# A two-layer residual kernel: VectorE adds the bias of another sequence of each group, at another place in its order

## The chip, the cores and the metric

The kernel runs on one core of a Trainium2 chip. A core has TensorE (PE in the profile), which multiplies matrices into the PSUM banks; VectorE (DVE), ScalarE (ACT) and GpSimd (POOL), which work elementwise; and SyncE (SP), which here only issues DMAs. Each engine runs its own instructions in order, and they wait for one another through semaphores. The metric is device time in microseconds (us): the median over the runs of one kernel.

## The reference, cut to what matters

There are 64 sequences of 128 rows and 512 columns, in float32. Two layers follow each other, each with a residual:

```
attn   = tanh(x @ W1 + b1); scores = attn @ v
p      = softmax(scores under a prefix, postfix or cloze mask, chosen per sequence)
x      = x + (p @ x) / cnt                       # first layer
x      = x + (x @ W[cat] + b[cat])               # second layer, W and b chosen per sequence
```

## The kernel before, in words

**The products.** With M the 128x128 matrix I + p/cnt of a sequence, the output is M @ (x @ (W[cat] + I)) plus the bias row b[cat]. So each sequence k needs x @ (W + I), called `xw(k)`, and then M @ that, called `pz(k)`; both sum into the same PSUM bank `ps_y`, of which there are five. Every float32 operand is split into a rounded high part and the remainder (`_hi` and `_lo`, float32r), and three products of the parts stand for one: 12 matmuls for `xw`, 3 for `pz`.

**The groups.** The sequences come in 16 groups of four; b = k % 4 is the place in the group. W1, the scores, the softmax and the transposed M are computed once for a group (`hidden`, `scores_group`, `exp_group`, `scale_group`, `transpose_probs`, `split_mix`). The order of every engine is written out by hand: a prologue, and then a loop over k in which each step of an engine stands where the code puts it. TensorE's iteration k does `xw(k)`, `pz(k-2)`, and for b = 0 the transposes, for b = 1 `hidden(g+1)` and for b = 2 `scores_group(g+1)`.

**Who does what.** W comes in 1 MB loads into five `w_raw` buffers. The identity is added to it by VectorE (`add_identity`, L466), for b = 1 and 2 by GpSimd (L282). ScalarE rounds it (`split_w_hi`, L346), and VectorE takes the remainder (`split_w_lo`, L479). The same pair works on x for `hidden` (L336, L472), on the first product (`z_hi` L382, `z_lo` L507), on the attention vector (`av_hi` L354, `av_lo` L484) and on the mixing matrix (`mix_hi` L375, `mix_lo` L502). GpSimd's second identity of a group waits for `av_lo`, its first for a `w_lo`. Further links of the softmax are VectorE's masked maximum (L492), ScalarE's exponentials (L361), GpSimd's `row_div` (L324), VectorE's reciprocal `row_scale` (L498) and ScalarE's scaling (L368).

**The bias.** For three sequences of a group the bias is a fourth matmul of `pz` (L695), and ScalarE copies the bank to `out_sb` (`copy_out`, L388). For one of them, the one with b = `WIDE`, SP loads the bias row into `out_sb[WIDE]`, spread over 128 partitions (`load_wide`, L240), and VectorE's `add_wide` (L514) adds the bank to it; then `pz` has three matmuls and ScalarE copies nothing. `wait_out` sends whoever needs the result (the store of k on SP, L234, and `xw(k+5)` on TensorE, which reuses the bank) to the right semaphore.

**SP's queue.** At t it issues `store(t-3)`, for b = 3 `load_x(g+3)` (1 MB, L230), `load_wide(g)` at its place, and `load_w(t+7)` (L219), which waits until the `w_lo` that used that buffer is done.

Of the kernel before, what the change touches and what calls it, by code (L numbers as in the profile page):

```python
# [39 lines left out]
def program(nc, xg, ids, w1, w, bias, out):  # L40
    GROUPS, P, DC, GS = xg.shape
# [6 lines left out]
    assert A == P and w1.shape[1] == DC * A + 2 and D == DC * P and C == P // 2  # L48
    HALF = DC // 2
    NX, NT, NW, NH, NL, NZ, NO, NY = 3, 2, 5, 4, 3, 3, 4, 5  # L50
    WIDE = 1
    assert NO == G
    RAW = 6

# [1 line left out]
    with ctx:  # L56
# [120 lines left out]
        def w_count(k):  # L177

            return k - RAW + 1
# [5 lines left out]
        def by_pool(k):  # L185

            return k > 3 * G and k % G in (1, 2)
# [9 lines left out]
        def wide(k):  # L197
            return k % G == WIDE

        def wait_out(engine, k):  # L200

            if wide(k):
                engine.wait_ge(sum_ready, k // G + 1)
            else:
                engine.wait_ge(out_ready, k - (k + G - WIDE - 1) // G + 1)

        @block.sync
        def _(sp):
            def load_cat(k):
                return sp.value_load(ids_row[0:1, k:k + 1], min_val=0, max_val=C - 1)  # L210

            def load_w(k, cat=None):
                if cat is None:
                    cat = load_cat(k)
                if k - NW >= RAW:
                    sp.wait_ge(w_lo_ready, w_count(k - NW))
                elif k >= NW:
                    sp.wait_ge(xw_done, k - NW + 1)
                sp.dma_start(w_raw[k % NW][:], w[bass.ds(cat, 1)].rearrange("a p c h -> p (a c) h"))\  # L219
                    .then_inc(w_in[k % NW], 16)  # L220

            def load_x(g):
                if g == NX:
                    sp.wait_ge(xw_done, G)
                elif g > NX:
                    if g == NX + 1:
                        sp.wait_ge(xw_done, RAW)
                    sp.wait_ge(xT_lo_ready, g - NX)
                    sp.wait_ge(pre_done, g - NX + 1)
                sp.dma_start(x_raw[g % NX][:], xg[g]).then_inc(x_in[g % NX], 16)  # L230

            def store(k):
                wait_out(sp, k)
                sp.dma_start(out[k], out_sb[k % NO][:]).then_inc(out_stored[k % NO], 16)  # L234

            def load_wide(g):
                cat = load_cat(G * g + WIDE)
                if g >= 1:
                    sp.wait_ge(out_stored[WIDE], 16 * g)
                sp.dma_start(out_sb[WIDE][:], bias[bass.ds(cat, 1), :].to_broadcast([P, D])).then_inc(wide_in, 16)  # L240

            sp.dma_start(ids_row[:], ids.rearrange("(a n) -> a n", a=1)).then_inc(ids_in, 16)
            for h, c in enumerate(halves):
                sp.dma_start(x_raw[0][:, c, :], xg[0][:, c, :]).then_inc(x0_in[h], 16)
            sp.wait_ge(ids_in, 16)
            cat_2 = load_cat(2)
            sp.wait_ge(w_in[0], 16)
            load_w(2, cat_2)
            load_x(1)
            load_w(3)  # L250
            sp.dma_start(b_raw[0:C, :], bias).then_inc(b_low_in, 16)
            sp.dma_start(b_raw[C:P, :], bias).then_inc(b_high_in, 16)
            load_w(4)
            load_w(5)
            load_x(2)
            load_w(6)
            load_wide(0)

            for t in range(B + 3):
                g, b = t // G, t % G  # L260
                if t >= 3:
                    store(t - 3)
                if b == 3 and g + 3 < GROUPS:
                    load_x(g + 3)
                if b == 2 and 1 <= g < GROUPS:
                    load_wide(g)
                if t + 2 + NW < B:
                    load_w(t + 2 + NW)
            for slot in range(NO):
                sp.wait_ge(out_stored[slot], 16 * (B // NO + (1 if slot < B % NO else 0)))  # L270
# [59 lines left out]
        def _(act):  # L330
# [40 lines left out]
            def split_mix_hi(g):  # L371
                act.wait_ge(probsT_done, g + 1)
                if g >= 2:
                    act.wait_ge(pz_done, G * (g - 1))
                nc.scalar.activation(mix_hi[g % 2][:], ps_pT[:].rearrange("p (b j) -> p b j", b=G), ACT.Copy)\  # L375
                    .then_inc(mix_hi_ready, 1)

            def split_z_hi(k):
                act.wait_ge(xw_done, k + 1)
                if k >= NZ:  # L380
                    act.wait_ge(pz_done, k - NZ + 1)
                nc.scalar.activation(z_hi[k % NZ][:], ps_y[k % NY][:], ACT.Copy).then_inc(z_hi_ready, 1)  # L382

            def copy_out(k):
                act.wait_ge(pz_done, k + 1)
                if k >= NO:
                    act.wait_ge(out_stored[k % NO], 16 * (k // NO))
                nc.scalar.activation(out_sb[k % NO][:], ps_y[k % NY][:], ACT.Copy).then_inc(out_ready, 1)  # L388
# [27 lines left out]
            split_z_hi(4)  # L416
            split_w_hi(6)
            split_mix_hi(1)
            copy_out(2)
            split_z_hi(5)  # L420
            split_w_hi(7)
            copy_out(3)
# [8 lines left out]
            for k in range(2 * G, B + 3):  # L431
                g, b = k // G, k % G
# [20 lines left out]
        def _(dve):  # L453
            eye = ident[:].rearrange("p (a j) -> p a j", a=1)

            def diagonal(slot):
                return w_raw[slot][:].rearrange("p c (i j) -> p (c i) j", j=P)[:, ::DC + 1, :]
# [6 lines left out]
            def add_identity(k):  # L464
                dve.wait_ge(w_in[k % NW], 16 * (k // NW + 1))
                nc.vector.tensor_tensor(diagonal(k % NW), diagonal(k % NW), eye.to_broadcast([P, DC, P]), ALU.add)\  # L466
                    .then_inc(wi_ready, 1)

            def split_xT_lo(g):
                dve.wait_ge(xT_hi_ready, g)  # L470
                cols = split_columns(g)
                nc.vector.tensor_tensor(xT_lo[g % NT][:, :, cols], x_raw[g % NX][:, :, cols],  # L472
                                        xT_hi[g % NT][:, :, cols].bitcast(F32), ALU.subtract).then_inc(xT_lo_ready, 1)

            def split_w_lo(k):
                dve.wait_ge(w_hi_ready, w_count(k))
                if k - NL >= RAW:
                    dve.wait_ge(xw_done, k - NL + 1)
                nc.vector.tensor_tensor(w_lo[k % NL][:], w_raw[k % NW][:], w_hi[k % NH][:].bitcast(F32),  # L479
                                        ALU.subtract).then_inc(w_lo_ready, 1)  # L480
# [15 lines left out]
            def row_scale_group(g):  # L496
                dve.wait_ge(div_ready, g + 1)
                nc.vector.reciprocal(row_scale[:], row_div[:]).then_inc(scale_ready, 1)  # L498

            def split_mix_lo(g):  # L500
                dve.wait_ge(mix_hi_ready, g + 1)
                nc.vector.tensor_tensor(mix_lo[g % 2][:], ps_pT[:].rearrange("p (b j) -> p b j", b=G),  # L502
                                        mix_hi[g % 2][:].bitcast(F32), ALU.subtract).then_inc(mix_lo_ready, 1)
# [6 lines left out]
            def add_wide(g):  # L510
                k = G * g + WIDE
                dve.wait_ge(pz_done, k + 1)
                dve.wait_ge(wide_in, 16 * (g + 1))
                nc.vector.tensor_tensor(out_sb[WIDE][:], ps_y[k % NY][:], out_sb[WIDE][:], ALU.add)\  # L514
                    .then_inc(sum_ready, 1)
# [57 lines left out]
            add_identity(6)  # L573
            row_scale_group(1)
            split_xT_lo(2)
            add_wide(0)
            add_identity(7)
            split_z_lo(4)
            split_w_lo(6)
            split_mix_lo(1)  # L580
            add_identity(8)
            split_w_lo(7)
            split_z_lo(5)
# [10 lines left out]
            for k in range(2 * G, B + 1):  # L594
                g, b = k // G, k % G
                if b == 3 and g + 1 < GROUPS:
                    max_group(g + 1)
                if b == 1 and g + 1 < GROUPS:
                    split_xT_lo(g + 1)
                if k + 2 < B:  # L600
                    split_w_lo(k + 2)
                if b == 1 and g < GROUPS:
                    split_mix_lo(g)
                if b == 2 and g + 1 < GROUPS:
                    split_av_lo(g + 1)
                split_z_lo(k - 1)
                if b == 0:
                    add_wide(g - 1)
                if k + 4 < B and not by_pool(k + 4):
                    add_identity(k + 4)  # L610
                if b == 3 and g + 1 < GROUPS:
                    row_scale_group(g + 1)

        @block.tensor
        def _(pe):
# [151 lines left out]
```

## Time and profile before

| | |
|---|---|
| median of 3 runs | 310.32 us (310.23 to 310.41) |
| the profiled execution | 311.67 us, of which 309.9 us are the span of the trace |
| TensorE busy | 302.9 us, 98% |
| VectorE busy | 278.1 us, 90% |
| ScalarE busy | 262.3 us, 85% |
| GpSimd busy | 86.0 us, 28% |
| DMA | 105.69 MB, mean 341 GB/s |
| chain that ended last | TensorE 88%, "issue" 6% |

The span is the time from the first to the last record of the core. The busy share of TensorE counts matmuls whose records overlap, so that it says little on how closely they follow one another; the distance between two starts says that. From about 60 us on, until 285 us, every group repeats the one before it.

### The profile page before, as it was taken

The page shows a single profiled execution, that of the slowest core. Times are in us where ns is not written, and L with a number is a line of the kernel's source. Part 1 is how long each engine was busy: PE and PEld are TensorE (multiplying, and loading weights), DVE is VectorE, ACT ScalarE, POOL GpSimd, SP SyncE. Part 2 cuts the span into 40 slices and gives each one's busy share as a digit, 9 for nine tenths or more (in the row PEclk, how much of TensorE's full clock was granted, in tenths as well). Part 3 has the DMA queues.
Part 4 walks back from the last instruction along what each step waited for, and adds up shares of the span by engine and source line. Part 5 has one row for each costly group of instructions (what it writes and reads, how often), then busy time and mean ns, then how long its engine had stood idle before and what let it go on. Part 6 is the DMA issues. An engine that isn't in the chain of part 4 may idle for free.

```text
span 309.9 us, 4890 instructions
## 1 busy us (share of the span) xinstructions
PE 302.9 (98%) x1284; PEld 233.7 (75%) x1284; DVE 278.1 (90%) x385; ACT 262.3 (85%) x429; POOL 86.0 (28%) x119
## 2 busy tenths in 40 slices
PE   8999999899999999999999999999999999999995
PEld 4445478588787878878788887888878787887884
DVE  4247699999999999999999999999999999999961
ACT  2254978989999898999989899998999999899952
POOL 5020400334132243413234341323424133302100
PEclk9999999999999999999999999999999999999999
DMA  7999899999999999999999999999999999986133
GB/s 257 404 389 412 339 403 379 415 396 295 352 373 318 404 320 401 363 354 373 327 406 319 408 350 361 361 322 409 323 392 349 370 378 334 399 327 224 67 135 135
DMA packets 23516, 105.69 MB, mean 341 GB/s; under 512 B 2625, under 2 KB 2626, under 8 KB 13378
## 3 DMA queue, kind: packets, MB, share of 16 engines
q1 hardware_dynamic: 23058, 103.03, 89.3%
q10 hardware_dynamic: 432, 2.36, 1.9%
q8 instruction: 10, 0.16, 0.2%
q14 instruction: 16, 0.13, 0.1%
HBM read 88.61 MB, written 16.78 MB: 340 GB/s over the span
## 4 chain that ended last, share of the span: by engine, by line
PE 88%; issue 6%; ACT 2%; DMA 2%; POOLq 1%; DVE 0%; SPq 0%; POOL 0%; ACTq 0%
PE ps_y L677 17%; PE ps_y L679 17%; PE ps_y L678 17%; PE ps_pre L636 13%; PE ps_y L689 4%; PE ps_y L690 4%; PE ps_y L691 4%; PE ps_y L695 3%; PE ps_pT L653 2%; PE ps_y L665 2%; PE ps_pre L625 2%; DMA x_raw<-in_x 2%; PE ps_scores L646 1%; PE ps_scores L644 1%; ACT probs L361 1%
## 5 line engine op out<-in xcount | busy, mean ns | idle before, releaser
L479 DVE TENSOR_TENSOR w_lo<-w_raw,w_hi 128x2048 fp32r<-128x2048 f32 x58 | 135.1, 2330 | 0.9 <-ACT w_hi L346 0.9
L346 ACT ACTIVATE w_hi<-w_raw 128x2048 fp32r<-128x2048 f32 x58 | 111.6, 1926 | 7.5 <-POOL w_raw L282 7.5
L677 PE MATMUL ps_y<-w_hi,xT_hi 128*128 128x512 f32 x232 | 91.7, 395 | 0.0
L679 PE MATMUL ps_y<-w_hi,xT_lo 128*128 128x512 f32 x232 | 90.5, 390 | 0.0
L678 PE MATMUL ps_y<-w_lo,xT_hi 128*128 128x512 f32 x232 | 90.3, 389 | 0.0
L282 POOL TENSOR_TENSOR w_raw<-w_raw,ident 128x512 f32<-128x512 f32 x26 | 33.6, 1294 | 113.5 <-DVE w_lo L479 75.0
L679 PEld LDWEIGHTS ps_y<-w_hi,xT_lo 128*128 128x128 f32 x232 | 43.5, 188 | 9.4
L507 DVE TENSOR_TENSOR z_lo<-ps_y,z_hi 128x512 fp32r<-128x512 f32 x64 | 43.7, 684 | 7.7 <-ACT z_hi L382 7.7
L678 PEld LDWEIGHTS ps_y<-w_lo,xT_hi 128*128 128x128 f32 x232 | 43.6, 188 | 8.8
L382 ACT ACTIVATE z_hi<-ps_y 128x512 fp32r<-128x512 f32 x64 | 38.8, 607 | 13.3 <-PE ps_y L679 5.1
L677 PEld LDWEIGHTS ps_y<-w_hi,xT_hi 128*128 128x128 f32 x232 | 43.6, 188 | 8.6
L289 POOL COPY mask<-penalty 128x128 bf16 x64 | 43.9, 716 | 9.4 <-issue 9.3
L472 DVE TENSOR_TENSOR xT_lo<-x_raw,xT_hi 128x2048 fp32r<-128x2048 f32 (+1 forms) x15 | 33.2, 2214 | 0.3 <-ACT xT_hi L336 0.3
L388 ACT ACTIVATE out_sb<-ps_y 128x512 f32<-128x512 f32 x48 | 29.0, 605 | 2.0 <-PE ps_y L695 2.0
L324 POOL TENSOR_TENSOR row_div<-row_sum,seen 128x4 f32<-128x4 f32 x16 | 6.4, 398 | 81.3 <-ACT probs L361 81.3
L336 ACT ACTIVATE xT_hi<-x_raw 128x2048 fp32r<-128x2048 f32 (+1 forms) x15 | 28.1, 1870 | 0.0
L689 PE MATMUL ps_y<-z_hi,mix_hi 128*128 128x512 f32 x64 | 25.9, 405 | 0.1
L466 DVE TENSOR_TENSOR w_raw<-w_raw,ident 128x512 f32<-128x512 f32 x37 | 25.3, 684 | 0.0
L690 PE MATMUL ps_y<-z_hi,mix_lo 128*128 128x512 f32 x64 | 24.9, 389 | 0.0
L691 PE MATMUL ps_y<-z_lo,mix_hi 128*128 128x512 f32 x64 | 24.9, 389 | 0.0
L352 ACT ACTIVATE attn<-ps_pre,w_pack 128x512 f32<-128x512 f32 x16 | 11.0, 690 | 15.8 <-PE ps_pre L625 8.0
L361 ACT ACTIVATE probs<-ps_scores,neg_max 128x128 f32<-128x128 f32 x64 | 22.4, 362 | 2.2 <-DVE neg_max L492 2.2
(70 smaller groups left out, 378.3 us busy)
## 6 DMA issues: line engine op xcount, KB each, us to landing
w_raw<-in_L_cond_W SPq DMA_DIRECT2D x62, 1024.0 KB, 8.4
out<-out_sb SPq DMA_DIRECT2D x64, 256.0 KB, 6.2
x_raw<-in_x SPq DMA_DIRECT2D x15, 1024.0 KB, 7.3
out_sb<-in_L_cond_b SPq DMA_DIRECT2D x16, 256.0 KB, 5.6
w_raw<-in_L_cond_W ACTq DMA_DIRECT2D x2, 1024.0 KB, 7.5
x_raw<-in_x SPq DMA_DIRECT2D x2, 512.0 KB, 5.2
w_pack<-in_W_b_v ACTq DMA_DIRECT2D x1, 257.0 KB, 2.8
b_raw<-in_L_cond_b SPq DMA_DIRECT2D x2, 128.0 KB, 8.2
```

The source lines that it names most:

```text
L289: last = nc.gpsimd.tensor_copy(mask[g % 2][:, i:i + 1, :], penalty[:, bass.ds(kind, 1), :])
L346: nc.scalar.activation(w_hi[k % NH][:], w_raw[k % NW][:], ACT.Copy).then_inc(w_hi_ready, 1)
L382: nc.scalar.activation(z_hi[k % NZ][:], ps_y[k % NY][:], ACT.Copy).then_inc(z_hi_ready, 1)
L479: nc.vector.tensor_tensor(w_lo[k % NL][:], w_raw[k % NW][:], w_hi[k % NH][:].bitcast(F32), ALU.subtract).then_inc(w_lo_ready, 1)
L507: nc.vector.tensor_tensor(z_lo[k % NZ][:], ps_y[k % NY][:], z_hi[k % NZ][:].bitcast(F32), ALU.subtract).then_inc(z_lo_ready, 1)
L636: last = nc.tensor.matmul(ps_pre[:], wp[:, c, :], xp[g % NT][:, c, :], start=(c == 0 and i == 0), stop=(c == DC - 1 and i == 2))
L677: nc.tensor.matmul(y[:], xT_hi[q][:, c, xs], w_hi[k % NH][:, c, :], start=(c == 0), stop=False)
L678: nc.tensor.matmul(y[:], xT_hi[q][:, c, xs], w_lo[k % NL][:, c, :], start=False, stop=False)
L679: last = nc.tensor.matmul(y[:], xT_lo[q][:, c, xs], w_hi[k % NH][:, c, :], start=False, stop=(c == DC - 1))
L689: nc.tensor.matmul(y[:], mh, z_hi[k % NZ][:], start=False, stop=False, skip_group_check=True)
L690: nc.tensor.matmul(y[:], ml, z_hi[k % NZ][:], start=False, stop=False, skip_group_check=True)
L691: last = nc.tensor.matmul(y[:], mh, z_lo[k % NZ][:], start=False, stop=wide(k), skip_group_check=True)
```

## The change

`WIDE` becomes 2, so that the bias that VectorE adds is that of each group's third sequence. Three things move with it: SP's `load_wide(g)` from b = 2 to b = 3, behind `load_x(g+3)`; ScalarE's `copy_out`, which now takes the sequence with b = 1 and leaves out the one with b = 2; and VectorE's `add_wide`, from the iteration with b = 0, behind `z_lo`, to the one with b = 1, behind `mix_lo` and `z_lo`. The fourth matmul of `pz` moves from the third sequence to the second. Nothing is added or removed.

```diff
-    WIDE = 1
+    WIDE = 2
@@ SyncE
                 if b == 3 and g + 3 < GROUPS:
                     load_x(g + 3)
-                if b == 2 and 1 <= g < GROUPS:
+                if b == 3 and 1 <= g < GROUPS:
                     load_wide(g)
@@ ScalarE, before the loop
             split_mix_hi(1)
-            copy_out(2)
+            copy_out(1)
@@ VectorE, before the loop
             split_xT_lo(2)
-            add_wide(0)
             add_identity(7)
             split_z_lo(4)
             split_w_lo(6)
             split_mix_lo(1)
+            add_wide(0)
             add_identity(8)
@@ VectorE, the loop
                 split_z_lo(k - 1)
-                if b == 0:
+                if b == 1:
                     add_wide(g - 1)
...
                     row_scale_group(g + 1)
+            add_wide(GROUPS - 1)
```

VectorE's order from the `z_lo` of the iteration with b = 0 to the `av_lo` of the one with b = 2, in the middle of the loop, before (the digit behind a name is its buffer):

```order
L507 TENSOR_TENSOR z_lo2<-ps_y3,z_hi2 128x512
L514 TENSOR_TENSOR out_sb1<-ps_y1,out_sb1 128x512
L466 TENSOR_TENSOR w_raw3<-w_raw3,ident 128x4x128
L472 TENSOR_TENSOR xT_lo1<-x_raw1,xT_hi1 128x2048
L479 TENSOR_TENSOR w_lo0<-w_raw2,w_hi3 128x2048
L502 TENSOR_TENSOR mix_lo0<-ps_pT,mix_hi0 128x512
L507 TENSOR_TENSOR z_lo0<-ps_y4,z_hi0 128x512
L479 TENSOR_TENSOR w_lo1<-w_raw3,w_hi0 128x2048
L484 SCALAR_TENSOR_TENSOR av_lo<-attn,w1_pack,av_hi 128x512
```

And the same stretch now:

```order
L507 TENSOR_TENSOR z_lo2<-ps_y3,z_hi2 128x512
L466 TENSOR_TENSOR w_raw3<-w_raw3,ident 128x4x128
L472 TENSOR_TENSOR xT_lo1<-x_raw1,xT_hi1 128x2048
L479 TENSOR_TENSOR w_lo0<-w_raw2,w_hi3 128x2048
L502 TENSOR_TENSOR mix_lo0<-ps_pT,mix_hi0 128x512
L507 TENSOR_TENSOR z_lo0<-ps_y4,z_hi0 128x512
L514 TENSOR_TENSOR out_sb2<-ps_y2,out_sb2 128x512
L479 TENSOR_TENSOR w_lo1<-w_raw3,w_hi0 128x2048
L484 SCALAR_TENSOR_TENSOR av_lo<-attn,w1_pack,av_hi 128x512
```

The add of L514 stood first among five instructions and stands now behind them; the `w_lo` in front of `av_lo` keeps its place in the sum.

ScalarE's order at the same time, from `xT_hi` to the `w_hi` behind `mix_hi`, now:

```order
L336 ACTIVATE xT_hi1<-x_raw2 128x2048
L388 ACTIVATE out_sb1<-ps_y3 128x512
L346 ACTIVATE w_hi3<-w_raw4 128x2048
L382 ACTIVATE z_hi1<-ps_y1 128x512
L375 ACTIVATE mix_hi0<-ps_pT 128x512
L346 ACTIVATE w_hi0<-w_raw0 128x2048
```

The copy of L388 stands in front of the first `w_hi`; before, it (of `out_sb2`) stood behind `mix_hi`.

SP's order from the store of the first sequence of a group, now (TENSOR_LOAD and the ISA rows read the category and set up the address):

```order
L234 DMA out<-out_sb0 128x512
L230 DMA x_raw2<-in_x 128x2048
L210 TENSOR_LOAD ids_row
L210 ISA x2
L240 ISA
L240 DMA out_sb2<-in_L1_cond_b 128x512
L210 TENSOR_LOAD ids_row
L210 ISA x2
L219 ISA
L219 DMA w_raw0<-in_L1_cond_W 128x2048
```

The load of L240 stood five rows in front of this store, ahead of the preceding `load_w`; now it is behind a load of x of 1 MB.

## Rows read from the trace of the kernel before

**Rows 1.** Chain that ended last: start us, us, what, xcount.

```profile
41.85 2.72 PE ps_pre L636 x12
...
61.17 0.62 issue
61.79 2.99 PE ps_pre L636 x12
...
279.51 2.88 PE ps_pre L636 x12
```

**Rows 2.** Waits, 70 to 285 us: engine line <- cause: us, times, longest.

```profile
PEld ps_pre L636 <- issue: 3.7, 12, 0.3
```

**Rows 3.** Timeline of VectorE: start us, us, engine, line, op, tiles.

```profile
59.41 2.28 DVE L472 TENSOR_TENSOR xT_lo<-x_raw,xT_hi 128x2048 fp32r<-128x2048 f32 x1
...
150.08 2.29 DVE L472 TENSOR_TENSOR xT_lo<-x_raw,xT_hi 128x2048 fp32r<-128x2048 f32 x1
...
155.69 2.48 DVE L479 TENSOR_TENSOR w_lo<-w_raw,w_hi 128x2048 fp32r<-128x2048 f32 x1
158.09 0.74 DVE L484 SCALAR_TENSOR_TENSOR av_lo<-attn,w_pack,av_hi 128x512 fp32r<-128x512 f32 x1
...
159.61 0.30 DVE L492 CUSTOM_DVE_ANT_0 ps_scores<-ps_scores,mask 128x128 f32<-128x128 f32 x1 [0.18 <-PE ps_scores L646]
...
164.15 0.18 DVE L498 RECIPROCAL row_scale<-row_div 128x4 f32<-128x4 f32 x1
...
167.03 0.68 DVE L514 TENSOR_TENSOR out_sb<-ps_y,out_sb 128x512 f32<-128x512 f32 x1
167.63 0.68 DVE L466 TENSOR_TENSOR w_raw<-w_raw,ident 128x512 f32<-128x512 f32 x1
...
170.43 2.29 DVE L479 TENSOR_TENSOR w_lo<-w_raw,w_hi 128x2048 fp32r<-128x2048 f32 x1
...
173.83 2.48 DVE L479 TENSOR_TENSOR w_lo<-w_raw,w_hi 128x2048 fp32r<-128x2048 f32 x1
```

**Rows 4.** Timeline of GpSimd.

```profile
154.72 1.30 POOL L282 TENSOR_TENSOR w_raw<-w_raw,ident 128x512 f32<-128x512 f32 x1 [5.49 <-DVE w_lo L479]
158.97 1.29 POOL L282 TENSOR_TENSOR w_raw<-w_raw,ident 128x512 f32<-128x512 f32 x1 [2.96 <-DVE av_lo L484]
163.69 0.43 POOL L324 TENSOR_TENSOR row_div<-row_sum,seen 128x4 f32<-128x4 f32 x1 [3.42 <-ACT probs L361]
```

**Rows 5.** Timeline of ScalarE.

```profile
160.30 1.92 ACT L346 ACTIVATE w_hi<-w_raw 128x2048 fp32r<-128x2048 f32 x1 [0.57 <-POOL w_raw L282]
...
167.42 1.93 ACT L346 ACTIVATE w_hi<-w_raw 128x2048 fp32r<-128x2048 f32 x1
...
170.18 0.62 ACT L388 ACTIVATE out_sb<-ps_y 128x512 f32<-128x512 f32 x1
170.66 1.96 ACT L346 ACTIVATE w_hi<-w_raw 128x2048 fp32r<-128x2048 f32 x1
```

**Rows 6.** All instructions of L479: duration ns min/median/max.

```profile
L479 DVE TENSOR_TENSOR w_lo<-w_raw,w_hi x58: 2276/2289/2485, 39.4 to 294.6; 128x2048 fp32r<-128x2048 f32 x58
```

**Rows 7.** Timeline of TensorE.

```profile
159.17 0.40 PE L646 MATMUL ps_scores<-av_lo,ones 128*128 128x512 f32 x1
```

**Rows 8.** Timeline of SP: start us, us to issue.

```profile
164.58 0.37 SPq L230 DMA_DIRECT2D x_raw<-in_x  x1
...
170.83 0.34 SPq L234 DMA_DIRECT2D out<-out_sb  x1
```

**Rows 9.** DMAs issued at 164.58, at 200.88 and at 299.35 us: KB, us to landing.

```profile
x_raw<-in_x SPq DMA_DIRECT2D x1, 1024.0 KB, 7.1
...
x_raw<-in_x SPq DMA_DIRECT2D x1, 1024.0 KB, 8.6
...
out_sb<-in_L_cond_b SPq DMA_DIRECT2D x1, 256.0 KB, 3.1
```

**Rows 10.** DMA issues of the page.

```profile
w_raw<-in_L_cond_W SPq DMA_DIRECT2D x62, 1024.0 KB, 8.4
```

## The prediction, made before the changed kernel ran

> **What bounds the kernel now.** I read the chain that ended last first. It runs through TensorE nearly all the way, and the reader is to look not at the share but at the twelve matmuls of `hidden` (L636). The first time that the split form runs, they take 2.72 us, 0.227 us each. From the next group on they take 2.88 to 2.99 us [rows 1]. The table of waits has a cause without a name for the weight load of these matmuls: 12 times, 3.7 us in total, 0.3 us each [rows 2]. VectorE's timeline gives it. In the first loop group `xT_lo` ends at 59.41 + 2.28 = 61.69 us, TensorE has been idle for 0.62 us, and `hidden` starts at 61.79 [rows 1, 3]. So TensorE waits for `xT_lo` once in every group, slightly, and loses about 2.89 - 2.72 = 0.17 us by it, since the weight load can't be done ahead.
>
> The period is (279.51 - 61.79) / 12 = 18.14 us a group [rows 1]. TensorE alone, without that loss, would need 18.14 - 0.17 = 17.97 us. What holds `xT_lo` back is a loop over the other engines, and I closed it from the timelines. `av_lo` ends at 158.83 [rows 3]. GpSimd adds an identity from 158.97 to 160.26, ScalarE rounds that W from 160.30 on and then does its exponentials, GpSimd's `row_div` runs from 163.69 to 164.12 [rows 4, 5], and VectorE's reciprocal starts at 164.15 [rows 3]: 5.32 us in which each step starts within 0.15 us of the one before. From there VectorE works without a gap to the next `av_lo`, which ends at 158.83 + 18.14 = 176.97: 12.82 us. 5.32 + 12.82 = 18.14 us, the whole period. VectorE's wait of 0.18 us for the scores [rows 3] lies within the 5.32 us and costs nothing.
>
> **The change part by part.**
>
> *The same work at another place.* One add of 0.68 us a group on VectorE, one copy of 0.62 us on ScalarE, one fourth matmul of 0.227 us and one load of 256 KB stay what they are [rows 3, 5]. From the sum they come out at nothing; only their places count. An add takes 0.60 us of VectorE's line, from 167.03 to 167.63 [rows 3].
>
> *`xT_lo` comes 0.60 us earlier.* The add now stands behind it. TensorE's wait of some 0.1 us before `hidden`, and the loss behind it, go. Worth 0.17 us a group, if the loop becomes as short as TensorE's 17.97.
>
> *A long `w_lo` becomes a normal one.* The add stays inside the loop, so moving it alone leaves 18.14. But of the 58 `w_lo` the median is 2.289 us and the longest 2.485 [rows 6], and the long one stands in the same place of each group, just ahead of `av_lo`: 155.69 and 173.83, both 2.48 us [rows 3]. At that time GpSimd's identity add runs, 154.72 to 156.02, started by the end of the previous `w_lo` [rows 4]. In the new order that previous `w_lo` ends, GpSimd starts about 0.15 us later and needs 1.30, so 1.45 us in all; VectorE meanwhile does `mix_lo`, `z_lo` and the bias add, 3 x 0.60 = 1.80 less the overlap of 0.09, and starts the critical `w_lo` 1.71 us after that end, when GpSimd is done. The loop loses 2.48 - 2.29 = 0.19 us. Bounds: nothing, if the length had another cause, and 0.19; I take it whole, since both long rows lie under GpSimd's add.
> The Trainium skill (GPSIMD Engine Reference, Specifications) says that GpSimd shares its SBUF interfaces with VectorE and that they get in each other's way when a VectorE instruction has two SBUF inputs. `w_lo` has two; `mix_lo`, `z_lo` and the bias add read one operand from PSUM. By that rule the three can stand under GpSimd's add at no cost, and the result is the one above; without it part of the 0.19 us would only move to the bias add.
>
> *ScalarE's copy in front of `w_hi`.* This speaks against the change. The copy takes about 0.48 us of ScalarE's line (170.18 to 170.66) and now stands ahead of the `w_hi` that starts at 167.42; that becomes 167.90 and ends at 169.83. Its `w_lo` stood at 170.43 and would now start at 169.83 [rows 3, 5]. With 0.03 us of signalling it waits 0.03 us. The margin of 1.1 us is used up, but not more. Bounds: 0 and 0.1 us a group.
>
> *New period.* The loop: 18.14 - 0.19 + 0.03 = 17.98; TensorE: 17.97. Two bounds that close get in each other's way now and then, and I take 18.00: 12 x 0.14 = 1.7 us. Bounds: 18.17 (no gain in the long `w_lo`), a loss of 0.4 us, and 17.97, a gain of 2.0.
>
> *Once, at the first loop group.* `hidden` can start at 61.2 instead of 61.79, a gain of 0.6 us. But the scores need `av_lo`, and there TensorE has a margin of only 159.17 - 158.83 = 0.34 us [rows 3, 7], plus 0.19 from the shorter `w_lo`. I take 0.45, bounds 0.3 and 0.6.
>
> *SP's queue and the weights.* The store of the third sequence, issued at 170.83 [rows 8], now waits for VectorE's add, which ends at about 173.9; behind it in the queue stands the load of a W, so that comes up to 3.1 us later. The weight's identity is added by VectorE three iterations, 13.6 us, after the `w_lo` that frees its buffer; 13.6 - 3.1 = 10.5 us against a median of 8.4 to land [rows 10]. Covered; if not, each late us stops VectorE for one.
>
> *The bias row behind x.* The row was asked for before x and is now asked for behind it. x is issued at 164.58 and lands 7.1 us later [rows 8, 9], at 171.7; a row of 256 KB needs about a quarter of the 2.5 to 3 us of a 1 MB load more, so it lands at about 172.4. The add wants it at 173.83 - 0.60 = 173.23 [rows 3]. The margin is 0.8 us. One x took 8.6 us [rows 9]; there the row would be about 0.7 us late, once. I charge 0.0 to 0.7, and take 0.1 in the sum.
> The Trainium skill (DMA: Bandwidth & Descriptors, Queues, rings and completion order) says that each DMA engine takes the descriptors of a ring in their order. By it the row can't pass x, which is what the margin above assumes.
>
> *The tail.* The last bias row was issued at 299.35 and took 3.1 us [rows 9]. It is now issued one store later, about 303, and lands at 306.1, some 0.5 us after its bank is ready; its store goes out just ahead of the last one. Between 0 and 0.5 us; I take 0.2.
>
> *Sum.* 1.7 + 0.45 - 0.1 - 0.2 = 1.85 us, about 1.9. The profiled execution has 309.9 us of span and 1.8 around it, 311.67; with the change 309.8. It lies 1.35 us above the median of the runs, so the median goes from 310.32 to 308.4.
>
> **The rivals.**
> 1. *The loop keeps its length.* The long `w_lo` stays long, or ScalarE's copy costs the 0.1 us a group. TensorE gains at the first group and then waits for `av_lo` instead of `xT_lo`: 12 x -0.03 + 0.3 - 0.3 = -0.4 to +0.2, so 310.1 to 310.7. For it: both new margins are below 0.1 us. Against it: the two long rows under GpSimd's add.
> 2. *The bias row comes late (slower).* VectorE's add stops for it in every group, and with it the loop, since nothing in it is slack. It decides from the point where the row lands more than 8.65 us after x is issued (173.23 - 164.58), and the change loses once the mean lateness is over 0.14 us. With 0.5 us late in each of 12 groups: 12 x (0.5 - 0.14) = 4.3, less 0.25 from both ends: about 314.4. For it: the 8.6 of one x, and that nothing stands ahead of the row but the longest load there is. Against it: the usual 7.1 leaves 0.8 us, and the W ahead of x no longer has the row in front of it.
> 3. *Half.* The row is late in some groups, or TensorE pays for waiting at the scores: half of the 1.7 us, about 309.3.
>
> **How the numbers follow.** My forecast 0.61, within 307.4 and 308.9; rival 3 0.12; rival 1 0.15; rival 2 0.12. The measurement tells a difference from none at about 0.2%, 0.6 us: faster is below 309.7, slower above 310.9. Faster: 0.61 + 0.11 + 0.01 = 0.73. Slower: rival 2 but for its smallest lateness, 0.10, and 0.01 of rival 1: 0.11. The same: 0.16. The range takes in the forecast and rivals 3 and 1, from 307.4 (17.97 a group and 0.6 at the start) to 310.8.
>
> **What would show it.** The twelve matmuls of `hidden` take 2.72 us in every group, and the waits of its weight load are gone. `w_lo` has no row above 2.35 us; GpSimd's first identity add ends before the `w_lo` ahead of `av_lo` starts. The period is 17.97 to 18.02 us. VectorE waits at most 0.1 us for `w_hi`, and not for a DMA in front of L514. I am wrong if L514 waits for the bias row in most groups (rival 2), or if the period stays at 18.1 with TensorE waiting at L646 (rival 1).

## The result, and the profile after

| | before | changed |
|---|---|---|
| median of 22 runs each | 310.28 us | 313.01 us |
| ratio (95% interval) | | 1.0053 (1.0037 to 1.007) |
| lowest run | 310.06 us | 309.80 us |
| span of the profiled execution | 309.9 us | 312.0 us |

The changed kernel is slower by 0.5%, about 1.6 us by the ratio, where I had forecast a gain, 308.4. Of the 22 runs of before all but two lie within 0.9 us; those of the changed kernel spread over 309.8 to 314.9, with two further outliers at 317.7 and 1078. The ratio leaves out the five slowest runs of the changed kernel as disturbed, of which three (314.6 to 314.9) only continue that spread, so it rather understates the loss; the medians over all runs lie 2.7 us apart. The profiled execution of the changed kernel took 313.79 us, 0.8 above its median.

The profile shows first what came as forecast. The twelve matmuls of `hidden` (L637 now, one line further down) in the chain, here those of the last group, to be held against [rows 1]:

```profile
281.31 2.73 PE ps_pre L637 x12
```

2.73 us, where they took 2.88. All `w_lo` (L479) of the changed kernel, as in [rows 6]:

```profile
L479 DVE TENSOR_TENSOR w_lo<-w_raw,w_hi x58: 2276/2286/2376, 37.8 to 296.8; 128x2048 fp32r<-128x2048 f32 x58
```

The maximum of 2.485 us is gone; the one ahead of `av_lo` takes 2.28. (The one `w_lo` of 2.376, at 54 us, lies just above the 2.35 that I had named as the limit.) Now VectorE's timeline of the changed kernel, its bias adds (L514) and its `av_lo` (L484), which [rows 3] show for before:

```profile
81.15 0.68 DVE L514 TENSOR_TENSOR out_sb<-ps_y,out_sb 128x512 f32<-128x512 f32 x1
83.94 0.75 DVE L484 SCALAR_TENSOR_TENSOR av_lo<-attn,w_pack,av_hi 128x512 fp32r<-128x512 f32 x1
99.13 0.68 DVE L514 TENSOR_TENSOR out_sb<-ps_y,out_sb 128x512 f32<-128x512 f32 x1
...
117.69 0.69 DVE L514 TENSOR_TENSOR out_sb<-ps_y,out_sb 128x512 f32<-128x512 f32 x1 [0.48 <-DMA out_sb<-in_L_cond_b]
...
172.38 0.68 DVE L514 TENSOR_TENSOR out_sb<-ps_y,out_sb 128x512 f32<-128x512 f32 x1
...
191.33 0.69 DVE L514 TENSOR_TENSOR out_sb<-ps_y,out_sb 128x512 f32<-128x512 f32 x1 [0.88 <-DMA out_sb<-in_L_cond_b]
...
210.23 0.69 DVE L514 TENSOR_TENSOR out_sb<-ps_y,out_sb 128x512 f32<-128x512 f32 x1 [0.82 <-DMA out_sb<-in_L_cond_b]
```

From 81.15 to 99.13 it is 17.98 us, the period that the loop was worked out to have. But where a bracket stands, the add waited for its bias row, and the group took 18.3 to 18.9 us, 18.56 for one (99.13 to 117.69). The waits of the changed kernel from 70 to 285 us, as in [rows 2]:

```profile
ACT w_hi L346 <- POOL w_raw L282: 13.8, 12, 1.7
PEld ps_scores L647 <- DVE av_lo L484: 6.0, 8, 1.1
...
DVE out_sb L514 <- DMA out_sb<-in_L_cond_b: 4.2, 8, 0.9
...
PE ps_scores L647 <- DVE av_lo L484: 2.3, 5, 0.7
```

The wait of the weight load for `hidden` is gone. In its place eight adds of twelve wait for a DMA, and TensorE waits behind them for `av_lo`, at the scores. The chain that ended last shows the whole way in one late group:

```profile
182.75 0.03 SPq L240
182.78 0.03 issue
182.81 8.43 DMA out_sb<-in_L_cond_b
191.24 0.03 issue
191.27 0.02 DVEq L513
191.29 0.04 issue
191.33 0.06 DVE out_sb L514
```

SP issues the row at 182.81, it lands at 191.24, and VectorE starts at once. The DMAs of this group, x issued at 181.67 and the row at 182.81, to be held against [rows 9]:

```profile
x_raw<-in_x SPq DMA_DIRECT2D x1, 1024.0 KB, 7.7
...
out_sb<-in_L_cond_b SPq DMA_DIRECT2D x1, 256.0 KB, 8.4
```

x lands at 189.4 and the row 1.9 us later. In the group before, x was issued at 163.67 and took 7.6 us, the row was issued at 165.46 and took 6.5: 0.6 us behind x, and in time. Over the eleven groups of the loop that load an x, the row landed 0.6 to 2.2 us behind it, 1.8 in the median, and x itself took 6.9 to 7.9 us. Counted from the issue of x, the row landed after 9.05 us in the median.

Twelve periods, from the `av_lo` of the first loop group to that of the last, took 285.02 - 67.40 = 217.6 us before and 286.81 - 65.95 = 220.9 us now.

### The profile page after: what moved, and what is told of

It is laid out like the page before. It is cut to its first block, busy times and chain, and to the rows that moved or that the text cites. A ratio compares the mean times of both kernels' runs of the same rounds, so it can differ in the third digit from the quotient of the medians.

```text
span 312.0 us, 4890 instructions
## 1 busy us (share of the span) xinstructions
PE 302.8 (97%) x1284; PEld 233.5 (75%) x1284; DVE 278.9 (89%) x385; ACT 262.2 (84%) x429; POOL 87.4 (28%) x119
## 2 busy tenths in 40 slices
DMA packets 23516, 105.69 MB, mean 339 GB/s; under 512 B 2625, under 2 KB 2626, under 8 KB 13378
## 4 chain that ended last, share of the span: by engine, by line
issue 28%; DMA 22%; PE 14%; DVE 12%; ACT 12%; POOL 5%; SPq 4%; POOLq 2%; ACTq 0%; DVEq 0%
DMA out_sb<-in_L_cond_b 20%; ACT probs L361 6%; DVE w_lo L479 5%; POOL w_raw L282 5%; DVE av_lo L484 3%; PE ps_y L678 3%; PE ps_y L679 3%; PE ps_y L680 3%; DMA w_raw<-in_L_cond_W 2%; ACT out_sb L388 2%; ACT w_hi L346 2%; SPq L210 2%; POOLq L288 1%; PE ps_y L666 1%; ACT probs L368 1%
## 5 line engine op out<-in xcount | busy, mean ns | idle before, releaser
L479 DVE TENSOR_TENSOR w_lo<-w_raw,w_hi 128x2048 fp32r<-128x2048 f32 x58 | 132.6, 2287 | 1.9 <-ACT w_hi L346 1.9
L289 POOL COPY mask<-penalty 128x128 bf16 x64 | 47.4, 769 | 11.7 <-issue 11.5
L388 ACT ACTIVATE out_sb<-ps_y 128x512 f32<-128x512 f32 x48 | 28.7, 598 | 2.0 <-PE ps_y L696 2.0
L324 POOL TENSOR_TENSOR row_div<-row_sum,seen 128x4 f32<-128x4 f32 x16 | 4.3, 270 | 79.8 <-ACT probs L361 79.8
L637 PE MATMUL ps_pre<-xT_hi,w_hi 128*128 128x512 f32 x56 | 21.9, 391 | 0.0
```

The lines of the kernel that those rows point to most:

```text
L289: last = nc.gpsimd.tensor_copy(mask[g % 2][:, i:i + 1, :], penalty[:, bass.ds(kind, 1), :])
```

## The experiments

My theory after the result: the new order on the engines does what the prediction says, and the late bias row alone costs more than it gives. The rival: the DMAs can't follow the shorter period, and the row is only the first to be late.

**e1, the row in front of x.**

```diff
+                if b == 3 and 1 <= g < GROUPS:
+                    load_wide(g)
                 if b == 3 and g + 3 < GROUPS:
                     load_x(g + 3)
-                if b == 3 and 1 <= g < GROUPS:
-                    load_wide(g)
```

> The changed kernel with the bias row asked for in front of the x of the same step instead of behind it; nothing else moves. Theory 1 (only the row's place in SP's queue costs): the row lands 6 us after its issue or less, well ahead of L514; no group waits for it, each takes 17.99 us as the three undisturbed groups of the changed kernel did (81.15, 99.13 us), and the time is 12 x 0.15 + 0.3 = 2.1 us below the kernel before: 308 to 308.6, with the runs within 0.5 us of one another. Theory 2 (the DMAs as a whole can't follow the shorter period, and the row is only the first to be late, since stores and weight loads now come in bursts): something else waits for a DMA, an x or a W, and the time is 310.5 to 313, scattered as in the changed kernel.

Measured: 308.98 us against 310.40 of before, ratio 0.9952 (0.9935 to 0.997). No add of the loop waits for a DMA; the last one of the kernel waits 1.1 us. Two of GpSimd's identities do wait for a W, 6.9 us together by GpSimd's own waits; one period, with the first of these waits in it, is 18.20 us, all others are 17.98 to 18.00. So theory 1 holds for the loop, but the time is 0.4 us above its range, the runs spread over 1.15 us instead of 0.5, and the two waits for a W are a trace of what theory 2 named.

**e2, the row early, in a buffer of its own.**

```diff
-                    sp.wait_ge(out_stored[WIDE], 16 * g)
-                sp.dma_start(out_sb[WIDE][:], ...
+                    sp.wait_ge(sum_ready, g)
+                sp.dma_start((b_raw if g else out_sb[WIDE])[:], ...
@@
-                if b == 3 and 1 <= g < GROUPS:
+                if b == 2 and 1 <= g < GROUPS:
                     load_wide(g)
@@ add_wide
+                if g >= 1:
+                    dve.wait_ge(out_stored[WIDE], 16 * g)
-                ... ps_y[k % NY][:], out_sb[WIDE][:], ALU.add)
+                ... ps_y[k % NY][:], (b_raw if g else out_sb[WIDE])[:], ALU.add)
```

> The changed kernel with the bias row asked for at the step where the kernel before asked for it (b = 2), into a buffer of its own (b_raw, free by then), so that the earlier place waits for no store. Theory 1: as the row in front of x, 308 to 308.6; the row lands some 10 us before L514 wants it. Theory 2: 310.5 to 313. A third possibility: SP's order with the row at b = 2 keeps x where it was, so if this one is faster than the row in front of x, x's own landing mattered.

Measured: 308.39 us, ratio 0.9928 (0.9914 to 0.9943), the six runs within 0.5 us. The `av_lo` of its first and last loop group:

```profile
65.90 0.74 DVE L484 SCALAR_TENSOR_TENSOR av_lo<-attn,w_pack,av_hi 128x512 fp32r<-128x512 f32 x1
...
281.81 0.75 DVE L484 SCALAR_TENSOR_TENSOR av_lo<-attn,w_pack,av_hi 128x512 fp32r<-128x512 f32 x1
```

(281.81 - 65.90) / 12 = 17.99 us, and no period is further from it than 17.98 to 18.02. The rows land 5.7 to 7.4 us before their adds (not 10, as expected), the last one 1.1 us before. In the loop nothing waits for a DMA, though all of them are there: this is where theory 2 falls. It is the engine order that the prediction described, without a late row, and the fastest kernel here. The 0.6 us between it and e1 are not x's landing, the third possibility: in the traces 0.57 of them lie behind the last `av_lo`, where e1's last add waits for its row.

The changed kernel's 220.9 us for the same stretch are 4.9 more than e2's 215.9 (one trace each). The waits of the adds account for them: eight waits of 4.2 us, and at each the 0.09 us by which an instruction of VectorE otherwise starts ahead of the recorded end of the one before it (99.13 to 117.69 is 18.56, 0.57 above 17.99, for a wait of 0.48). 4.2 + 8 x 0.09 = 4.9. That is what the late rows cost.

**e3, no rows.**

```diff
-                if b == 3 and 1 <= g < GROUPS:
-                    load_wide(g)
@@ add_wide
-                dve.wait_ge(wide_in, 16 * (g + 1))
+                dve.wait_ge(wide_in, 16)
+                if g >= 1:
+                    dve.wait_ge(out_stored[WIDE], 16 * g)
```

> The changed kernel without the bias rows of groups 1 to 15 (the bias of those 15 sequences is left out; the add itself stays). It bounds what all the row's DMAs can cost: theory 1 expects 308 to 308.6, the same as the row in front of x within 0.3 us. Theory 2 expects a further gain over the row in front of x, or no gain at all if it is the stores and W loads that come late.

Measured: 308.46 us, ratio 0.9933 (0.9917 to 0.9949). Taking fifteen DMAs of 256 KB away (3.9 of 105.69 MB) gives no more than landing them in time, as theory 1 expected.

**e4, the row one load further back.**

```diff
-                if b == 3 and 1 <= g < GROUPS:
-                    load_wide(g)
                 if t + 2 + NW < B:
                     load_w(t + 2 + NW)
+                if b == 3 and 1 <= g < GROUPS:
+                    load_wide(g)
```

> The changed kernel with the row asked for behind the W of the same step, one 1 MB load further back. Theory 1: its landing moves back by one W, about 2.5 us, L514 waits in every group for 2 to 3 us, and the loop with it: 12 x 2.5 = 30 us more than the undisturbed kernel, about 335 to 340. Theory 2: no more than 2 us above the changed kernel's 313.

Measured, one run: 334.25 us. Two of its adds:

```profile
164.89 0.69 DVE L514 TENSOR_TENSOR out_sb<-ps_y,out_sb 128x512 f32<-128x512 f32 x1 [2.27 <-DMA out_sb<-in_L_cond_b]
...
185.18 0.69 DVE L514 TENSOR_TENSOR out_sb<-ps_y,out_sb 128x512 f32<-128x512 f32 x1 [2.20 <-DMA out_sb<-in_L_cond_b]
```

185.18 - 164.89 = 20.29 us, 2.30 more than 17.99, for a wait of 2.2 to 2.3: each late us is a us of the period. The time is just below the 335 to 340 of theory 1, far from the 315 of theory 2.

**e5, GpSimd's add back under `w_lo`** (from e2).

```diff
                 if k % G == 1:
-                    pool.wait_ge(w_lo_ready, w_count(k - 2))
+                    pool.wait_ge(z_lo_ready, k - 4)
```

> The kernel with the row in its own buffer (the one with the row at b = 2, 308.4 us), in which GpSimd's first identity add of a group waits for the z_lo two instructions behind the w_lo that it waited for. It then starts about 1.2 us later and lies under the w_lo ahead of av_lo again. If GpSimd's add is what stretches w_lo, that w_lo goes from 2.28 us to 2.6 or more (before, 0.3 us of overlap made 2.48), and the period from 17.99 to 18.2 or 18.3, for 12 groups 2.5 to 4 us: 311 to 312.5. If the stretch had another cause: w_lo stays at 2.28, and the time at 308.4.

Measured: 318.80 us against 310.79 of before, ratio 1.0253 (1.0228 to 1.0278), much more than expected. GpSimd's add, and VectorE's bias add (L516 here) and `w_lo`, in one group:

```profile
157.06 1.30 POOL L282 TENSOR_TENSOR w_raw<-w_raw,ident 128x512 f32<-128x512 f32 x1 [5.83 <-DVE z_lo L507]
```

```profile
156.83 0.68 DVE L516 TENSOR_TENSOR out_sb<-ps_y,b_raw 128x512 f32<-128x512 f32 x1
157.43 3.08 DVE L479 TENSOR_TENSOR w_lo<-w_raw,w_hi 128x2048 fp32r<-128x2048 f32 x1
```

They overlap from 157.43 to 158.36, 0.93 us, and `w_lo` takes 3.08 instead of 2.28: VectorE loses 0.80 us. Before, it was 0.33 us of overlap and 0.20 lost. The bias add, with one operand in PSUM, keeps its 0.68 us under the first 0.45 us of GpSimd's; in e2, where GpSimd's add runs from 152.09 to 153.39, `mix_lo`, `z_lo` and the bias add lie under it and take 0.68 us each. The period becomes 18.79 (157.06 to 175.85 on GpSimd). The cause of the long `w_lo` is shown. The Trainium skill (GPSIMD Engine Reference, Specifications) names as contending with GpSimd VectorE's instructions with two SBUF inputs, and those in a 2-port mode, which no run here looks at. For the first this trace agrees, 3.08 us against an unchanged 0.68.

**e6, ScalarE's copy behind `mix_hi`** (from e2).

```diff
-                if not wide(k - 3):
+                if b in (2, 3) or k == B:
                     copy_out(k - 3)
+                elif b == 1 and k < B:
+                    copy_out(k - 4)
```

> The kernel with the row in its own buffer, with ScalarE's copy of the second sequence moved from in front of the w_hi (b = 0) to behind mix_hi (b = 1), where the kernel before had its copy. If that copy holds w_hi and so w_lo up: VectorE's gap of 0.09 us in front of that w_lo goes, the period falls from 17.99 to TensorE's own 17.97 or below, and the time by 0.2 to 0.5 us to 308.0. If TensorE bounds already: 308.4, unchanged.

Measured: 308.72 us, ratio 0.9919 (0.9899 to 0.9939). Its `xT_lo` and `w_lo`:

```profile
165.93 2.38 DVE L474 TENSOR_TENSOR xT_lo<-x_raw,xT_hi 128x2048 fp32r<-128x2048 f32 x1
168.23 2.28 DVE L481 TENSOR_TENSOR w_lo<-w_raw,w_hi 128x2048 fp32r<-128x2048 f32 x1
```

The gap in front of `w_lo` is gone, but `xT_lo` is 0.09 us longer; it starts 0.23 us before the end of GpSimd's copies of the mask (L289, 162.66 to 166.16), and where that overlap is 0.10 to 0.17 us, as mostly in the changed kernel, `xT_lo` takes 2.29 to 2.31. No run tests that cause. The ratio is not told from that of e2. The copy's place costs nothing that can be measured: the periods are 17.91 to 18.03 us, 17.98 in the mean, against 17.99 in e2.

**e7, only `xT_lo` ahead of the add** (from the kernel before).

```diff
                 if b == 1 and g + 1 < GROUPS:
                     split_xT_lo(g + 1)
+                if b == 1:
+                    add_wide(g - 1)
...
-                if b == 0:
+                if k == B:
                     add_wide(g - 1)
```

> The kernel before (WIDE = 1, the row at its old place) with one edit: in the loop VectorE's bias add stands behind xT_lo instead of in front of it. TensorE's wait for xT_lo goes, but the add stays ahead of the previous w_lo, so that GpSimd's add still overlaps the long w_lo. If the loop over GpSimd and ScalarE sets the period (my reading of the profile), it stays 18.14 and the time stays at 310.3, less at most 0.4 from the first group. If TensorE's wait for xT_lo is itself the bound (the simple reading), the period falls to 17.97 and the time to about 308.3.

Measured: 310.01 us against 310.79 of before, ratio 0.9974 (0.9957 to 0.999). The waits and one `w_lo`:

```profile
PEld ps_scores L648 <- DVE av_lo L484: 3.3, 12, 0.3
```

```profile
154.85 2.48 DVE L479 TENSOR_TENSOR w_lo<-w_raw,w_hi 128x2048 fp32r<-128x2048 f32 x1
```

TensorE's wait for `xT_lo` is gone, and twelve waits at the scores stand in its place, 3.3 us in all. The period is (284.00 - 66.73) / 12 = 18.11 us, by the first and last `av_lo`. So the wait that the profile shows on the busiest engine was not the bound; the loop was. Taking the wait away gives 0.03 us a period, a fifth of the gain; the other 0.12 come with the shorter `w_lo`. Not its whole 0.20: 18.11 - 0.20 would be 17.91, less than the 17.97 that the prediction gives TensorE alone.

**e8, another source for the row** (from the changed kernel).

```diff
-                ... bias[bass.ds(cat, 1), :].to_broadcast([P, D])).then_inc(wide_in, 16)
+                ... xg[0][:, 0, :]).then_inc(wide_in, 16)
```

> The changed kernel with the row's DMA reading a block of x, 128 different rows of 2 KB, instead of one row of the bias 128 times; same size, same place, same target (the added bias is another number). If the repeated reading of one row makes it slow behind x: the row lands 0.7 us after x (as 256 KB do by size) instead of the 1.6 that the late groups show, and most waits of L514 go, about 310. If the place alone does it: it lands 1.2 to 2.2 us after x as before, and L514 waits in some 8 groups, about 313.

Measured, one run: 312.10 us. Over the eleven groups the block landed 1.4 to 2.1 us behind x, 1.6 in the median, and five adds waited for it, not some eight. In one group x was issued at 162.99 and took 7.4 us, the block at 164.22 and took 7.8: 1.6 us behind. That 128 partitions read one row is not the reason, or not much of it.

**e9, W held until the row has landed** (from the changed kernel).

```diff
                 if t + 2 + NW < B:
+                    if b == 3 and 1 <= g < GROUPS:
+                        sp.wait_ge(wide_in, 16 * (g + 1))
                     load_w(t + 2 + NW)
```

> The changed kernel in which SP issues the W behind the bias row only when the row has landed. It asks why the row lands 1.5 us behind x, the median of 11 groups, when 256 KB behind a 1 MB load would need 0.6 to 0.7. If the W behind it shares the DMA engines with it: the row lands 0.5 to 0.9 us behind x in nearly all groups, and L514 waits for it hardly at all. If x itself leaves the engines unevenly, or the row is slow in itself: still 1.2 to 2.2 us. The total is not the point: that W comes some 5 us later and may hold GpSimd's add up, 310 to 325.

Measured, one run: 335.98 us; its late W stop GpSimd ten times from 70 to 285 us, 48.4 us in all, so the total says nothing on the row. L514 waits once in that stretch, 0.2 us. What it was asked for is x issued at 153.29 and the row issued at 154.44:

```profile
x_raw<-in_x SPq DMA_DIRECT2D x1, 1024.0 KB, 8.1
...
out_sb<-in_L_cond_b SPq DMA_DIRECT2D x1, 256.0 KB, 7.6
```

161.4 and 162.0: 0.6 us behind x. Over the eleven groups it is 0.6 to 0.8 us. So the other 1.1 us of the median come with the W of 1 MB that SP issues 1.1 us behind the row. The packets show it at work before the row is complete: a W is 128 packets of 8 KB, a row or a store 128 of 2 KB. Between the landing of x and that of the row, in the changed kernel from 189.37 to 191.24 us and in e9 from 161.39 to 162.02:

```profile
DMA packets 152, 0.74 MB, mean 396 GB/s; under 512 B 15, under 2 KB 15, under 8 KB 77
```

```profile
DMA packets 4, 0.01 MB, mean 10 GB/s; under 512 B 1, under 2 KB 1, under 8 KB 4
```

x has landed, so the 152 - 77 = 75 packets of 8 KB are the W's; in e9 there is none. In the two groups of the changed kernel whose row landed 0.6 us behind x, W's packets were moving too (31 in 0.6 us); why those rows were done early all the same, no run shows. (The expectation above gives the changed kernel's lag as 1.5 us; counted over its groups the median is 1.8.)

**e10, the row from ScalarE's queue** (from the changed kernel, groups 3 to 15).

```diff
+                if b == 3 and 3 <= g < GROUPS:
+                    load_wide_act(g)       # as load_wide, issued by ScalarE
                 if b != 3 and k + 3 < B:
```

> The changed kernel with the bias rows of groups 3 to 15 issued from ScalarE's queue instead of SP's, at the same time as x (behind the copy of the first sequence). If a row is late because it stands behind x in one queue: it now lands ahead of x, 3 to 5 us after its issue, and L514 waits for no DMA. If all transfers in flight share the engines whatever their queue: it lands 6 us or more after its issue, with x or behind it. Reading the category costs ScalarE about 0.7 us in its tightest stretch, ahead of w_hi, so the period grows by 0.5 to 1 us, to 314 to 320, for that reason alone.

Measured, one run: 308.64 us, and no add of the loop waits for a DMA (the last one of the kernel waits 0.9 us). The time that was expected, 314 to 320, was wrong, and so was a landing after 3 to 5 us. ScalarE's queue issued the row at 159.06, ahead of its exponentials (from 159.76) and of the copy behind which it is written (161.12), so it was asked for 2 us earlier than meant and 3.1 us ahead of x (162.20). It landed ahead of x, but this doesn't tell whether another queue lets it pass x; it took 6.6 us in the median. Reading the category cost nothing that the time shows: the periods are 17.99 to 18.01 us, and the queue ran ahead of the engine. As a kernel whose rows are in time, e10 agrees with e2 and e3.

## Why the prediction was wrong, point by point

- *The loop of 18.14 us and its two parts.* Right but for 0.03 us: e7 takes TensorE's wait away and the period becomes 18.11, where the loop alone was to keep it at 18.14. (5.32 + 12.82 = 18.14 proves nothing by itself, since the 12.82 was got by taking 5.32 from the period; what carries it is that VectorE's rows have no gap there.)
- *`w_lo` shorter by 0.19 us.* Right, and its cause is shown by e5.
- *ScalarE's copy.* Right that it costs next to nothing (e6). The gap that it leaves in front of `w_lo` is 0.09 us, not 0.03.
- *New period, 18.00.* Right for a group that isn't late: 17.98 and 17.99. Whether the loop or TensorE holds it there, no run separates.
- *At the first group, 0.45 us.* Too much. From the first masked maximum (L492) to the first loop `av_lo` it is 67.40 - 15.58 = 51.82 us before, 65.90 - 14.26 = 51.64 in e2: 0.2 us. The profiled execution of before was itself 1.3 us later at that maximum, 15.58 against 14.28 in the changed kernel, ahead of any instruction that the change moves.
- *The weights behind the later store.* Right: neither in the changed kernel nor in e2 does any engine wait for a W in the loop.
- *The tail.* About right: 309.9 - 285.02 = 24.9 us from the last `av_lo` before, 25.2 in the changed kernel; 24.8 in e2, which asks for the row earlier. The last add waited 1.0 us in the changed kernel.
- *The bias row behind x.* This step failed. It said: "a row of 256 KB needs about a quarter of the 2.5 to 3 us of a 1 MB load more, so it lands at about 172.4", a margin of 0.8 us, and charged 0.1 us in the sum. The row landed 1.8 us behind x in the median, not 0.7. I took the DMAs of one queue to finish one after the other at full rate, for the last bytes too. e9 shows 0.6 us only where nothing is behind the row; with a W behind it the row waits longer, 1.1 us more than the step gave it. x itself took 7.6 us in the median (7.3 before), where the step had taken one row of 7.1. So the row landed 9.05 us after the issue of x, not 7.8, and the add wants it after 8.65. The term measured 4.9 us (e2 against the changed kernel), in place of 0.1. That the row doesn't pass x was right: it landed behind x in all eleven groups.

Without that term the sum was good: e2 lies 2.0 us below before, the sum without its 0.1 for the row had 1.95. That it fits so closely is in part luck: the first group was put 0.25 too high, and the tail, charged with 0.2, gained 0.1 in e2.

Rival 2 was the nearest, with its rule (loop and lateness add up, and the change loses from a mean lateness of 0.14 us on). The adds were late by 4.9 us in sum, by their own waits: 4.9 / 12 = 0.41 us a group, 0.27 over the 0.14 that the order gives, and 12 x 0.27 = 3.2 us for the stretch, where 220.9 - 217.6 = 3.3 were measured. It had the add stop in every group; it stopped in eight of twelve, which is how rival 3 described it, but rival 3 kept half of the gain. I gave rival 2 a chance of 0.12, with the one x of 8.6 us as its only support, and had no row of before in which a short DMA stood between two long ones.

## What to carry to other kernels

When a transfer is moved in a queue, give it the landing time of its neighbours there, the ones behind included, and not the time of its own bytes behind the one ahead: here 1.8 us in the median instead of 0.6. A small load that an engine in the critical loop waits for goes ahead of the large ones, in a buffer that lets it be asked for early. And before believing a small wait on the busiest engine, close the loop over the other engines: here the wait was only where the loop showed.

## What I had not expected of the hardware

- A VectorE instruction of two SBUF inputs that starts under GpSimd's elementwise add loses nearly the whole overlap: 0.80 us of 0.93, 0.20 of 0.33, so 0.13 us less than the overlap both times. GpSimd's own instruction keeps its 1.30 us. But a `w_lo` that has started before GpSimd's bf16 copies of the mask (L289) come under it keeps its length: in e2 the copies run from 162.11 to 165.51 us, and the `w_lo` of 161.88 takes 2.27.
- A 256 KB load between two of 1 MB landed 0.6 to 2.2 us after the first, and 0.6 to 0.8 us with the second held back. The spread of single runs went with it: 0.5 us over six runs in e2, 5 us over twenty of the changed kernel's 22.
